# A decoder on one Trainium2 core: dividing the self attentions' outputs by their sums in feature layout, after a trip through DRAM

## The reference, cut to what matters

```python
x = x + _L0_attn_ref(_layernorm(x, axis=-1), L0_attn_w_attn, L0_attn_w_proj)      # causal
...
x = x + _L1_attn_ref(_layernorm(x, axis=-1), L1_attn_qkv_w, L1_attn_proj_w, ...)  # no mask, RMS norm on q and k

# in both, per batch and head:
att = jax.nn.softmax(q @ k.T / sqrt(16), axis=-1)
y = att @ v                      # (512, 16)
out = concat_heads(y) @ w_proj.T
```

## Time and profile before

| | |
|---|---|
| median of 3 runs | 2590.68 us (2586.22 to 2602.6) |
| the profiled execution, its own time | 2594.22 us |
| its span | 2592.5 us |
| busy over the span: PE, PEld | 2344.4 us (90%), 1527.6 us (59%) |
| busy: DVE, ACT, POOL | 1456.5 us (56%), 1138.4 us (44%), 734.1 us (28%) |
| DMA | 148.85 MB, mean 57 GB/s |
| mean granted TensorE clock | 0.957 |

### The profile page before, as it was taken

How to read it: one execution, slowest core, us unless ns; L and a number is a source line. 1 busy time by engine, 2 the same in 40 slices (tenths; PEclk the granted TensorE clock), 3 DMA queues, 4 the chain that set the end, 5 groups by cost and what they waited for, 6 DMA issues and landing times. The chain is left out here.

```text
span 2592.5 us, 45640 instructions
## 1 busy us (share of the span) xinstructions
PE 2344.4 (90%) x14600; PEld 1527.6 (59%) x14613; DVE 1456.5 (56%) x3885; ACT 1138.4 (44%) x2683; POOL 734.1 (28%) x848
## 2 busy tenths in 40 slices
PE   7999999889996798899999999878897699999998
PEld 5455555545565566643343443445556499999997
DVE  4776676437764444477777777355545733434433
ACT  1665566523331443267777776522232033333332
POOL 3111111044422311233322221153321333333333
PEclk8999999999997899999999999999995899999999
DMA  6222222110000310312212122100008222222221
GB/s 155 87 87 93 82 82 81 56 49 5 5 1 7 110 32 1 80 63 74 69 56 75 63 66 71 38 9 9 9 1 324 91 33 35 36 35 36 36 34 23
DMA packets 135325, 148.85 MB, mean 57 GB/s; under 512 B 25286, under 2 KB 119152, under 8 KB 135024
## 3 DMA queue, kind: packets, MB, share of 16 engines
q1 hardware_dynamic: 119270, 126.44, 15.7%
q0 software_dynamic: 13680, 17.84, 4.3%
q10 hardware_dynamic: 2202, 2.39, 0.5%
HBM read 100.71 MB, written 46.01 MB: 57 GB/s over the span
## 5 line engine op out<-in xcount | busy, mean ns | idle before, releaser
L452 ACT ACTIVATE self_probs<-self_score_ps 128x512 f32<-128x512 f32 (+3 forms) x1024 | 481.0, 516 | 315.0 <-PE self_score_ps L813 162.7
L618 DVE TENSOR_REDUCE self_neg_max<-self_max_ps 128x1 f32<-128x512 f32 x512 | 328.2, 685 | 148.0 <-PE self_max_ps L799 143.5
L799 PE MATMUL self_max_ps<-self_k_stack,self_q_stack 96*128 96x512 bf16 (+3 forms) x1024 | 348.3, 342 | 21.6 <-DVE self_neg_max L615 12.1
L810 PE MATMUL self_score_ps<-self_q_stack,self_k_stack 99*128 99x512 bf16 (+3 forms) x1024 | 342.4, 342 | 1.6 <-ACT self_probs L452 1.6
L2256 ACT ACTIVATE x_stream<-experts_up_ps,experts_bias_now 128x128 f32<-128x128 f32 x568 | 162.5, 369 | 387.6 <-PE experts_up_ps L2477 387.6
L615 DVE CUSTOM_DVE_ANT_0 self_masked<-self_max_ps,self_later 128x128 f32<-128x128 f32 (+3 forms) x512 | 235.5, 488 | 124.5 <-PE self_max_ps L799 113.1
L2477 PEld LDWEIGHTS experts_up_ps<-experts_tileT,x_stream 128*128 128x128 f32 x2272 | 266.8, 193 | 5.1 <-issue 1.6
L2477 PE MATMUL experts_up_ps<-experts_tileT,x_stream 128*128 128x128 f32 x2272 | 267.3, 276 | 1.2 <-DVE x_stream L2393 1.2
L2487 PE MATMUL experts_down_ps<-experts_down,x_stream 128*128 x1136 | 256.8, 379 | 0.0
L824 PE MATMUL self_out_ps<-self_probs,self_values 128*32 128x512 f32 (+3 forms) x2048 | 231.8, 524 | 3.3 <-ACT self_probs L452 1.4
L810 PEld LDWEIGHTS self_score_ps<-self_q_stack,self_k_stack 99*128 99x128 bf16 x1024 | 98.9, 97 | 229.1 <-ACT self_probs L452 171.1
(11 more groups left out here) (293 smaller groups left out, 3977.4 us busy)
## 6 DMA issues: line engine op xcount, KB each, us to landing
self_parts_dram<-self_parts SPq DMA_DIRECT2D x64, 384.0 KB, 2.3
self_q_stack<-self_parts_dram SPq DMA_DIRECT2D x384, 64.0 KB, 2.3
self_k_stack<-self_parts_dram SPq DMA_DIRECT2D x360, 64.0 KB, 2.3
experts_up<-moe_up_dram SPq DMA_DIRECT2D x8, 1024.0 KB, 8.3
experts_down<-moe_down_dram SPq DMA_DIRECT2D x8, 1024.0 KB, 10.8
x_stream<-x_dram SPq DMA_DIRECT2D x8, 512.0 KB, 8.0
expert_rows_dram<-experts_down SPq DMA_DIRECT2D x8, 512.0 KB
out_dram<-x_stream SPq DMA_DIRECT2D x8, 512.0 KB, 8.4
```

Of the source, the lines that this page charges most:

```text
L452: act.activation(probs[:, i % 8, 0:w], score_ps[:, (16 * n + i) % 3, 0:w], ACT.Exp).then_inc(exp_done, 1)
L618: dve.tensor_reduce(neg_max[:, n % 2, t, h:h + 1], max_ps[:, i % 2, 0:w], AX, ALU.max, negate=True).then_inc(max_read, 1)
L799: last = pe.matmul(max_ps[:, i % 2, 0:w], q_stack[0:ROWS, h, P * t:P * t + P], k_stack[0:ROWS, h, 0:w], start=True, stop=True)
L810: last = pe.matmul(score_ps[:, m % 3, 0:w], k_stack[0:KROWS, head, P * j:P * j + P], q_stack[0:KROWS, head, S - w:S], start=True, stop=not ...
```

## The change

The division by the sums is done in feature layout. A group's `o_raw` is stored to DRAM (`out_store`, SP). For each half batch (two groups, 8 heads), two loads bring it back (`out_load`, SP): one packs the 16 value rows of each of 8 heads into the 128 partitions of `o_now`, the other reads one row of sums for each head and writes it to that head's 16 partitions in `sums`. ACT inverts the sums in place by Ln and Exp with scale -1 (`inverted`), in the chunks (3, 0) and, for the second half, (1, 2) of the next batch; both functions are in the table set that is loaded anyway. DVE multiplies into `oT` (`normalise`), in (3, 2) and (1, 3). The side works "ot" and "ob", the copies of `turned_back` and the tiles `o_tok` and `r_sums` are gone. `copy_out` now waits until the store of two groups before has landed.

```diff
-            if j == 1 and n >= 1:
-                work.append(("ot", n - 1))
...
-                work += {(1, 1): [("ob", b - 1, 1)], (2, 0): [("e", b - 1, 0)], (2, 1): [("e", b - 1, 1)]}.get((g, j), [])
+                work += {(2, 0): [("e", b - 1, 0)], (2, 1): [("e", b - 1, 1)]}.get((g, j), [])
...
-            if (g, j) == (3, 1):
-                work.append(("ob", b, 0))
...
+                def out_store(n):
+                    b, g = n // NG, n % NG
+                    sp.wait_ge(o_copied, n + 1)
+
+                    wait(sp, out_loaded[g // 2], 32 * b)
+                    sp.dma_start(out_scratch[g // 2, GH * (g % 2):GH * (g % 2) + GH].rearrange("h c d t -> (h c d) t"),
+                                 o_raw[:, n % 2]).then_inc(out_stored[n % 2], 16)
+
+                def out_load(b, half):
+                    for i in range(2):
+                        sp.wait_ge(out_stored[i], 16 * (2 * b + half) + 16)
+
+                    wait(sp, o_done, 2 * (b - 1) + half + 1 if b else 0)
+                    sp.dma_start(o_now[:, half], out_scratch[half, :, 0]).then_inc(out_loaded[half], 16)
+                    sp.dma_start(sums[:, half], out_scratch[half, :, 1, 0:1].to_broadcast([2 * GH, HD, S])).then_inc(out_loaded[half], 16)
...
                 def copy_out(n):
                     act.wait_ge(pv_done, 4 * n + 4)
-                    wait(act, ot_full, n - 1)
+                    wait(act, out_stored[n % 2], 16 * (n // 2))
...
+                def inverted(b, half):
+                    act.wait_ge(out_loaded[half], 32 * b + 32)
+                    act.activation(sums[:, half], sums[:, half], ACT.Ln).then_inc(sums_logged, 1)
+                    act.wait_ge(sums_logged, 2 * b + half + 1)
+                    act.activation(sums[:, half], sums[:, half], ACT.Exp, scale=-1.0).then_inc(sums_inverted, 1)
...
                         if (g, j) == (1, 2) and b >= 1:
-                            turned_back(b - 1, 1)
+                            inverted(b - 1, 1)
...
-                        if (g, j) == (3, 2):
-                            turned_back(b, 0)
+                        if (g, j) == (3, 0):
+                            inverted(b, 0)
...
-                copy_out(N - 1)
-                turned_back(B - 1, 1)
+                inverted(B - 1, 1)
...
+                def normalise(b, half):
+                    dve.wait_ge(sums_inverted, 2 * b + half + 1)
+
+                    wait(dve, e_full, 2 * b)
+                    dve.tensor_tensor(oT[:, half], o_now[:, half], sums[:, half], ALU.mult).then_inc(o_done, 1)
...
-                    pe.wait_ge(ob_copied, 2 * b + 2)
+                    pe.wait_ge(o_done, 2 * b + 2)
```

More of the change, by code:

```diff
@@ L282, in _ @@
                     more = b + 1 < B
+                    if b >= 1:
+                        out_store(4 * b - 1)
                     place_shift(4 * b + 1)
+                    if b >= 1:
+                        out_load(b - 1, 1)
                     if more:
@@ L643, in between @@
                     if half == 0:
-                        if j == 2 and n >= 1:
-                            normalise(n - 1)
+                        if (g, j) == (3, 2):
+                            normalise(b, 0)
                         if (g, j) == (1, 3) and more:
@@ L668, in between @@
                             leftover(b + 1, 3)
+                        if (g, j) == (1, 3) and b >= 1:
+                            normalise(b - 1, 1)
                         if next2:
```

54 lines of the change are left out of this document (19 added, 35 removed).

## The result

The changed kernel takes 2605.6 us (median of 20 runs, 2596.93 to 2612.32), the kernel before, in the same comparison, 2599.3 us (20 runs, 2586.22 to 2605.26). The ratio is 1.0029 with a 95% interval of 1.0016 to 1.0041: the change makes the kernel slower by 0.3%, some 7.5 us by the ratio and 6.3 by the medians, inside the 1% that I called no change, but on the other side of zero from the forecast of -11 us. The three runs shown at first had a median of 2590.68; the twenty have one 8.6 us higher. So of the 26 us from the forecast of 2579.5 to 2605.6 a third is that the first three runs lay low among the twenty, and two thirds are the change.

A forecast was written before the change was run, and what follows sets the result against it. TensorE was taken to bound most of the norm stage, a chain over ACT and DVE the causal stage in places. Norm -13, causal -9, ends +11 give -11 us: 2583 profiled, 2579.5 median; range 2563 to 2602.

The forecast's parts named there:

- Four transposes, 0.44 us: TensorE, both stages: each four transposes removed save 0.44 us, 42 us for 96 fours if all passes through.
- The causal loop: Causal stage: 0.9 to 1.0 us less a batch, 9 us in all with the last batch.
- 1 us for the last batch, where there are no maxima: Causal stage's last batch: a gain of 1 us, counted within the 9 us.
- The norm loop: Norm stage: 1.8 us less a batch, 13 us over 8 batches, the first and last giving less.
- The 0.2 us for DVE's relief: Norm stage, (0, 2) and (2, 2): DVE loses its `normalise` there, taken as 0.2 us.
- the step that failed: Norm stage, (1, 1): 0.88 us of transposes go, but "mt" in (2, 0) is late next; 0.2 us gain taken.
- at 0 beyond the 0.7 us that I have kept back in (1, 1): ACT's added Ln and Exp pairs in (3, 0) and (1, 2): covered by side works, no further cost.
- It waits 1.13 us for POOL: Norm stage, "mt" in (2, 0): waits 1.13 us for POOL, whose work is released by ACT's second cut.
- The ends: Both stage ends: 9 us for the uncovered trip, 2 for the norm end's clock; 11 us more, between 6 and 16.
- 2.8 us: Stage ends: two loads, the second issued 0.5 us later, take 2.8 us, from a 2.3 us landing.
- The trip is late: Rival, chance 0.09: ACT waits for `sums` in (3, 0), hops taking 8.0 us for 2.3; about 2698 us.
- Nothing is left but the ends: Rival, chance 0.25: ACT's pairs and DVE waits eat the gain; +11 to +21 us, 2590 to 2612, likely 2598.

The follow-up runs named there:

- the second experiment: The changed kernel, with POOL cutting the last group's maxima before adding the next batch's bias, norm stage only: 2594.1 us, ratio 0.9991 to the kernel before.

## Why the prediction was wrong

It had most of the mechanisms, and the sign of the sum was wrong because its sizes were: the loops gave 6.1 us for 22, and the ends cost 14.0 for 11. Two things were missing altogether, the half clock inside the norm loop and what stands ahead of POOL's cuts. In its own steps:

- **"Four transposes, 0.44 us".** Right: (1, 1) of the norm stage lost 0.87 us for eight.
- **The causal loop, "0.9 to 1.0 us a batch", -9 in all.** The batch is right (0.95), and so is where: (0, 1) with (0, 2) 0, (3, 1) with (3, 2) 0 (2.55 and 4.99 for 3.50 and 4.04), (2, 1) 0.45 and (2, 3) 0.24, (1, 1) with (1, 2) 0.28. The sum is not: "1 us for the last batch, where there are no maxima" came out as a loss of 2.2 us, since there (3, 0) is short, Ln waits for the load, and PE waits for ACT's pair:

```profile
480.28 0.63 ACT L468 ACTIVATE self_sums<-self_sums 128x512 f32<-128x512 f32 x1 [0.65 <-DMA self_sums<-self_out_dram]
...
482.11 0.34 PE L819 MATMUL self_score_ps<-self_q_stack,self_k_stack 99*128 99x384 bf16 x1 [1.94 <-ACT self_probs L478]
```

  And I had counted eight batches where five are steady, the first gives nothing (51.85 for 51.88) and the seventh 0.7. So -3.2 for -9, the first mis-sized term.
- **The norm loop, "1.8 us a batch", -13 in all.** (0, 1) and (2, 1) gave 0.44 each and (3, 1) with (3, 2) 0.42, near the 0.5 forecast. The 0.2 us for DVE's relief were nothing: (0, 2) stayed at 4.56 and (2, 2) at 3.72. (1, 1) was the step that failed. I had named POOL's chain and left 0.2 us of gain; (1, 1) to (2, 0) together became 0.2 us longer, because ACT's pair pushes the chain back by 0.3 (the experiment without it). Then came the half clock, 1.65 us in three batches, which I had looked for only at the ends. So -2.9 for -13; 5 of the 10 missing us are the clock.
- **ACT "at 0 beyond the 0.7 us that I have kept back in (1, 1)".** Right in the steady causal batches, wrong in the last one, 0.3 us a batch in the norm loop.
- **"It waits 1.13 us for POOL".** I read the chain back to ACT's second cut and not to what POOL does between that and its cuts. The bias addition, 2.4 us there and 2.8 in the changed kernel, stands in their way; moving it was worth 10 to 11 us in either kernel, about what I had forecast for the whole change.
- **The ends, +11, "2.8 us" for the loads.** +14.0. The store took its 2.0 to 2.3 us; the first of two loads took 4.7 us and the pair 5.2 to 5.4, so that the projections stood 9.47 and 9.68 us behind the copies for the 7.5 of the forecast. I had put the median landing of a store into DRAM in the place of a pair of loads from it. What the runs show in its place is 5.2 to 5.4 us, with 0.51 of the DMA engines busy, and 0.26 with the load cut, where the store had 1.00 and a load of 512 KB of weights took 3.6 us. That the idle engines are the cause is likely and not shown; reading one row 16 times is ruled out. The Trainium skill's rule of a fixed part plus the bytes ("DMA: Bandwidth & Descriptors", Anatomy of one DMA), fitted there to DMAs issued from GpSimd, gives 2.6 us for 256 KB as the prediction estimated from it. That is nearer to the store (2.0 us to landing) than to these loads. The clock at the norm end came as forecast (1.8 us for the 2 taken), in part by luck, since it fell in two executions with the old division there as well. The 14.0 us lie inside the range of 6 to 16.
- **The trip is late**, 0.09: not in each batch, but it is not absent either. The 4.3 us of spare time came from the same 2.3 us of landing. In the changed kernel's causal loop, Ln of (3, 0) starts 5.7 to 6.9 us behind the first load's issue, so that against the 5.3 us of the ends 0.4 to 1.6 are to spare, and in six of ten traces they did not always do. In the steady norm loop there are 9.0 us, and 13.4 or more for the second half.
- **The rivals.** "Nothing is left but the ends" is nearest. Its text says +11 us, up to +21, and then most likely 2598, which is +7; the two don't fit each other, 2590.7 + 11 being 2602. The result, +7.5 us, came by another way: something was left of the loops, 6 us, and the ends cost more. That it lies near the 2598's +7 is luck.
- **The level.** I forecast an absolute time from three runs, whose median lay 8.6 us under that of twenty. From the twenty's 2599.3 the forecast would have been 2588, still 17 us under the result.

**Open.** The loop and ends of the second experiment's profiled execution add up to 7.7 us under the kernel before, the timed runs say 2.3 (up to 5.7). Loads that are late in some executions would do that, but this was not tried. What decides whether a wait of 1.68 us is followed by the half clock (three batches of five) is open too; waits of 1.43 and 1.13 us in the same place never were. And it is open what the ends would cost with the loads spread over all DMA engines.

## What to carry to other kernels

Work taken from a busy engine is worth what the next late chain leaves of it: follow that chain through every instruction of its engine before counting the gain, since one that nobody needs yet may be the whole wait. A trip through DRAM was free in a loop with 9 us between load and use, at risk with 6 or 7, and costs its full two hops where a stage ends, so the last iteration can keep the old way. Price a load by a load of its own shape, not by another transfer's median landing, and look at the busy share of the DMA engines while it runs: 0.5 can mean that half of them have no part in it. An experiment that halves the bytes and leaves the time alone shows little until one knows what else it halved.

## What the runs showed of the hardware

- A store of 256 KB to DRAM ran with all 16 DMA engines busy (share 1.00, 379 GB/s) and landed in 2.0 us. A pair of loads of 256 KB, written with 8 heads outermost, ran at a share of 0.51 and 193 GB/s and took 5.2 to 5.4 us from issue to the waiting engine's start; with 4 heads and half the bytes it ran at 0.26 and 97 GB/s and took 5.2 to 5.3. A load of 512 KB whose semaphore rises 16 times landed in 3.6 us.
- A stall of PE of 1.68 us inside full load was followed in three of five cases by some 3.4 us at 1.2 GHz, though PE worked again throughout (in six executions together, in 16 of 30 cases, always in the same three batches or the first of them); with fillers in the stall there was none. At the end of a stage 3.24 us with nearly nothing were not followed by it in one execution, 4.28 us were in another; but the clock also fell at the norm end of two executions in which PE had no wait over 1 us there.
- DVE's reciprocal over 128x512 took 3.35 us; Ln and Exp over the same on ACT 1.26 us.
- The same pair of loads inside the loop, behind and ahead of other transfers of its queue, took up to 8.1 us (267.35 to 275.48).
